# A graph network on one core: inverse root by a power on GpSimd, bias rows added by GpSimd and VectorE

## The chip, the cores and the metric

The kernel runs on one core of a Trainium2 chip. The metric is the device time of one execution in microseconds (us); the kernel before has a median of 6995.06 us over 3 runs (6994.69 to 6996.19). The engines are called TensorE (PE), VectorE (DVE), ScalarE (ACT), GpSimd (POOL) and SyncE (SP).

## The reference

6250 nodes with 256 numbers each, 106250 edges. Four layers, each followed by a residual and a LayerNorm over the 256 numbers:

```python
x = layernorm(x + L0(x))   # h = x @ hamilton(W0); out = segment_sum(edge_weight * h[src], dst)
                           # BatchNorm over the nodes, tanh
x = layernorm(x + L1(x))   # q, k, v = x @ W.T + b; 8 heads, softmax over each node's edges; @ Wo.T + bo
x = layernorm(x + L2(x))   # GAT, 4 heads, + b1; layernorm, relu; GAT, 1 head, + b2
x = layernorm(x + L3(x))   # GCN: segment_sum(dinv[src] * dinv[dst] * (x @ W.T)[src], dst) + b
                           # BatchNorm over the nodes, relu, + x
layernorm = (x - mean) * rsqrt(var + 1e-5)
```

All LayerNorms have the form in the last line (the one inside the GAT also a gain and an offset); the change is about how the `rsqrt` is taken, and about the rows `bq`, `bk`, `bv`, `bo`, `b1`.

## The kernel before

The kernel has a preparation and then five rounds, L = 0 to 4 (the GAT layer takes two rounds). Each round is an **edge pass** and a **node stage**, with a barrier of all five engines between them. In the edge pass GpSimd gathers rows of a table by indirect DMA, 128 edges at a time, TensorE sums them with one-hot matrices, and VectorE adds the sums into `acc`, which keeps the sums of all nodes in SBUF. The change leaves the edge passes alone but for a short preparation of weights at their start.

A node stage walks over the 49 tiles of 128 nodes (`NT`) in steps s; an operation with skew k works on tile n = s - k (`tiles(s, k)`), so each engine's program is a fixed round of operations on different tiles, in the order of its code. No planner is involved. The engines wait for each other by counting semaphores: `rr` (residual added), `var` (mean and variance there), `std` (root taken), `xn` (normalised), `xt` and `xtc` (transposed, copied to SBUF), `pj` (projected), `po` (table row ready), `ps` (stored).

- VectorE: in stages 1 and 2 it divides the sums by the softmax denominators (`pre`, line 1898), then adds the residual or bias (lines 1910, 1914, 1916, 1920), takes statistics (1941, 1936), a reciprocal of ScalarE's root (1933), and normalises (1924; in stages 3 and 4 ScalarE does that at 879, and VectorE makes its offset at 1928).
- ScalarE: `Sqrt` of variance + eps (874), copies of the transposed tile (897) and of the projections out of PSUM (906, 907, 911, 912). In stages 0 and 4 it also applies tanh or Relu to a chunk of four tiles every fourth step (`bend`, 856). Table loads stand in the trace as ACT_TABLE_LOAD.
- TensorE, stage 0: transposes of the layer's result (1185) and of the normalised tile (1208), then the projection onto K and V (1221, 512 columns), a product with `ones_b` and `b3` that adds their bias (1224), the projection onto Q (1227) and its bias (1228). Stage 1: transposes (1191), the product with Wo (1200), the bias row `bo` (1201), transposes (1208), the next layer's projection (1221). A float32 bias is split into three bfloat16 parts by `split_bias` (1386 to 1391), during the edge pass.
- GpSimd, stage 0: rounds the remainder of Q to bfloat16 (725). Stages 1 and 2: zeroes the tile of `acc` (733). Stage 3: adds the row `b2` to the residual tile (721), before VectorE needs it at 1903. Stage 4: nothing.
- SyncE stores the tables and residual tiles, and loads residual tiles in groups of 7.

In stage 0 the remainder of Q goes round three engines: ScalarE's 907 keeps the upper half, VectorE's 1950 subtracts it (semaphore `r0`), GpSimd rounds (725), VectorE's 1945 subtracts again (`qd`), and SyncE stores.

## Time and profile before

| | us |
|---|---|
| median of 3 runs | 6995.06 |
| the profiled execution, its own time | 6978.94 |
| span of that execution | 6977.1 |
| stages 0, 1, 2, 3, 4 (windows read below) | 204, 120, 88, 78, 66 |
| busy over the span: TensorE, VectorE, GpSimd, ScalarE | 4606.5, 4396.6, 4515.6, 2546.8 |

The five node stages together are 556 us, 8% of the span; the busy times over the whole span are those of the edge passes above all. So the rows are read by stage. "Idle before" is the engine's idle time just before the instructions of that group, with what ended it. PEclk is the granted TensorE clock as a share of 2.4 GHz. A row of a window has its stretch, its length, then for each engine the busy us and the count of instructions, then PEclk, the DMA engines' busy share and GB/s. A row of a group has line, engine, operation, output<-input, shapes and count, then busy us and mean ns, then idle before. A timeline row has start, duration, engine, line and operation.

### The profile page before, as it was taken

The numbers are of one execution on the slowest core, as the hardware profiler recorded it, in microseconds if no ns is written. First come the engines' busy times: TensorE is split into PE (matmuls) and PEld (weight loads), VectorE is DVE, ScalarE is ACT, GpSimd is POOL, SyncE is SP. The second block draws the span as 40 slices with busy tenths as digits, with TensorE's granted clock in tenths as the row PEclk, the third lists the DMA queues.
The fourth block names the chain that finished last, engine by engine and source line by source line (L and its number), as shares of the span: only waits on it lengthen the run. The fifth ranks groups of instructions, "written<-read, shape, count | busy, mean of one in ns | idle before, by whom it ended". The sixth has DMA issues, their size and how long they took to land.

```text
span 6977.1 us, 103168 instructions
## 1 busy us (share of the span) xinstructions
PE 4606.5 (66%) x17172; PEld 3026.2 (43%) x17173; DVE 4396.6 (63%) x11645; ACT 2546.8 (37%) x6805; POOL 4515.6 (65%) x4928
## 2 busy tenths in 40 slices
PE   3555555877777777784777777566776735555556
PEld 2444444544444444463444444444444423343333
DVE  5555554558888888874666666655565564444546
ACT  0000000545555655654555555554554540000004
POOL 5777776036666666617777775377777747777770
PEclk8777777988888878896777777777777767777776
DMA  3333335257777777745444444344444543333333
GB/s 86 105 105 105 105 104 102 90 189 221 222 219 222 219 222 223 214 123 149 137 131 132 132 131 92 99 133 135 131 131 136 119 137 105 105 105 105 105 103 89
DMA packets 499186, 962.75 MB, mean 138 GB/s; under 512 B 105403, under 2 KB 296510, under 8 KB 491616
## 3 DMA queue, kind: packets, MB, share of 16 engines
q0 software_dynamic: 240064, 696.46, 36.9%
q1 hardware_dynamic: 258749, 262.93, 11.6%
q14 instruction: 335, 2.74, 0.1%
q8 instruction: 38, 0.62, 0.0%
HBM read 895.74 MB, written 64.63 MB: 138 GB/s over the span
## 4 chain that ended last, share of the span: by engine, by line
PE 36%; POOL 20%; issue 18%; DVE 15%; DVEq 4%; DMA 4%; ACT 3%; ACTq 1%; POOLq 0%; SPq 0%
PE bank L977 21%; POOL ring L707 19%; DVE acc L1439 4%; PE bank L1027 3%; DMA ring<-g_t,stage 2%; PE bank L1221 2%; DVE ring L1651 2%; DVE acc L1436 2%; PE bank L1174 1%; DVE aux L1500 1%; PE bank L1042 1%; DVE ohc L1445 1%; PE bank L1043 1%; PE bank L1044 1%; PE bank L1200 1%
## 5 line engine op out<-in xcount | busy, mean ns | idle before, releaser
L977 PE MATMUL bank<-ring,ohc 128*128 128x256 f32 (+3 forms) x8800 | 3212.4, 517 | 1550.7 <-DMA ring<-xs_t,stage 432.4
L977 PEld LDWEIGHTS bank<-ring,ohc 128*128 128x128 f32 x8800 | 2063.5, 252 | 2500.1 <-issue 1066.7
L1439 DVE TENSOR_TENSOR acc<-acc,bank 128x256 f32 (+2 forms) x3520 | 1485.2, 422 | 1498.3 <-PE bank L977 1368.0
L707 POOL DMA_INDIRECT ring<-g_t,stage x1760 | 1715.7, 975 | 521.7 <-issue 466.2
L707 POOL DMA_INDIRECT ring<-kv_t,stage x880 | 918.2, 1043 | 555.3 <-PE bank L977 325.8
L707 POOL DMA_INDIRECT ring<-in_x,stage x880 | 835.2, 949 | 263.8 <-issue 256.7
L707 POOL DMA_INDIRECT ring<-xs_t,stage x880 | 834.1, 948 | 260.9 <-issue 258.3
L840 ACT ACTIVATE aux<-bank 128x512 f32<-128x512 f32 (+1 forms) x26 | 14.9, 572 | 2225.5 <-PE bank L1163 2225.5
L766 ACT ACTIVATE ohc<-iota,rel_c 128x128 f32<-128x128 f32 x1760 | 557.2, 388 | 67.7 <-PE bank L977 66.6
L812 ACT ACTIVATE cl<-cl 128x1 f32<-128x1 f32 (+3 forms) x111 | 22.5, 203 | 1502.6 <-DVE mx L1644 909.7
L1436 DVE SCALAR_TENSOR_TENSOR acc<-acc,aux,bank 128x264 f32 x880 | 422.9, 481 | 119.9 <-PE bank L977 106.8
L1651 DVE TENSOR_TENSOR ring<-ring 128x1024 f32<-128x1024 f32 (+1 forms) x495 | 487.4, 985 | 14.1 <-issue 5.7
L794 ACT ACTIVATE ring<-ring 128x32 f32<-128x32 f32 x1760 | 378.1, 306 | 0.0
L1445 DVE TENSOR_SCALAR ohc<-iota,rel_c,relx 128x128 f32<-128x128 f32 x883 | 321.0, 364 | 88.3 <-issue 88.3
L827 ACT ACTIVATE ring<-ring 128x256 f32<-128x256 f32 x880 | 353.9, 493 | 2.2
L1448 DVE TENSOR_SCALAR ohc<-iota,rel_c 128x128 f32<-128x128 f32 x883 | 273.9, 310 | 99.4 <-issue 99.4
L769 ACT ACTIVATE ohc<-ohc,onesm 128x512 f32<-128x512 f32 x440 | 317.6, 722 | 32.3
L1042 PE MATMUL bank<-acc,oht 128*128 x880 | 268.2, 305 | 38.7 <-DMA aux<-q_t 30.0
L1500 DVE TENSOR_TENSOR aux<-bank,ring 128x1024 f32<-128x1024 f32 x220 | 267.9, 1218 | 11.6 <-PE bank L1044 10.0
L1491 DVE TENSOR_REDUCE sc<-aux 128x32 f32<-128x1024 f32 x220 | 267.3, 1215 | 2.0
L1043 PE MATMUL bank<-acc,oht 128*128 x880 | 266.7, 303 | 0.0
L1044 PE MATMUL bank<-aux,oht 128*128 128x256 bf16 x880 | 261.0, 297 | 0.0
(299 smaller groups left out, 4954.1 us busy)
## 6 DMA issues: line engine op xcount, KB each, us to landing
aux<-relb_t SPq DMA_DIRECT2D x56, 1024.0 KB
aux<-q_t SPq DMA_DIRECT2D x880, 64.0 KB
relx<-relb_t SPq DMA_DIRECT2D x55, 512.0 KB
ring<-g_t,stage POOLq DMA_INDIRECT x1760, 2.8
x<-ring SPq DMA_DIRECT2D x21, 896.0 KB, 4.2
ring<-x SPq DMA_DIRECT2D x21, 896.0 KB, 9.5
mk<-mk SPq DMA_DIRECT2D x445, 32.1 KB
ring<-in_x,stage POOLq DMA_INDIRECT x880, 2.8
```

The source lines that it names most:

```text
L707: g_.indirect_dma_start(out=rings[L][:, slot, 0:W], out_offset=None, in_=table[L][:, :], in_offset=bass.IndirectOffsetOnAxis(ap=stage[:, s ...
L766: act.activation(ohc[:, at_k + j, :], iota[:, :], ACT.Abs, scale=-1.0, bias=rel_c[:, ds(c * G + 4 * g + j, 1)])
L794: ins = act.activation(part, part, ACT.Copy, scale=rg[:, cset * G + k, po_ + h:po_ + h + 1])
L827: ins = act.activation(row, row, ACT.Copy, scale=rg[:, rset * G + k, 256:257])
L977: return mm(agp[k % AB][:, 0:width], ohc[:, hot, :], rg[:, slot, vo:vo + width], start=True, stop=True)
L1042: mm(to, hot, accb[:, ds(at_ + 2 * AW, D)], start=True, stop=False)
L1043: mm(to, hot, accb[:, ds(at_ + (2 * AW + D), D)], start=False, stop=False)
L1436: v.scalar_tensor_tensor(win, win, same[:, ds(b * G + k, 1)], agp[k % AGP[L]][:, 0:width], ALU.mult, ALU.add).then_inc(p["added"], 1)
L1439: tt(win, win, agp[k % AGP[L]][:, 0:width], ALU.add).then_inc(p["added"], 1)
L1445: ins = v.tensor_scalar(ohc[:, k % 8, :], iota[:, :], rel, ew_c[:, ds(b * G + k, 1)], ALU.is_equal, ALU.mult)
L1500: tt(prod, qe4[r % 2].rearrange("p (t w) -> p t w", t=4), rg[:, rset * G + 4 * r:rset * G + 4 * r + 4, 0:256], ALU.mult).then_inc(p["prod" ...
L1651: return tt(vv, vv, wv, ALU.mult)
```

## The change

- The root moves. GpSimd takes variance + eps (a 128x1 `tensor_scalar`), drains, and raises it to -0.5 (`tensor_tensor` with `half` and `ALU.pow`) in all five stages. ScalarE's `Sqrt` and VectorE's reciprocal go; the steps behind move up by one.
- Stage 0: VectorE adds the bias row of K and V (`kv_b`, 128x512) while it takes the projection out of PSUM; ScalarE's copy (906) and TensorE's product (1224) go. VectorE's last subtraction (1945) moves to GpSimd.
- Stage 1: GpSimd adds `bo` to the residual tile (as stage 3 does with `b2`); TensorE's product (1201) goes. Stage 2: GpSimd adds `b1`, VectorE's 1916 goes, and VectorE's statistics wait for GpSimd.
- `split_bias` is left for the 256 columns of Q alone.

```diff
@@ gpsimd, node stage
-                for n in range(NT):
-                    if L == 3:
+                for s in range(NT + 9):
+                    n = tiles(s, 0)
+                    if n is not None and L == 3:
...
                         g_.tensor_tensor(X49[:, n, :], X49[:, n, :], vrow[:, :], ALU.add).then_inc(q["xb"], 1)
-                    if L == 0:
+                    m = tiles(s, (4, 5, 4, 3, 4)[L])
+                    if m is not None:
+                        pool.wait_ge(q["var"], through("var", L) + m + 1)
+                        pool.nop(nofuse=True)
+                        g_.tensor_scalar(lnst[:, m % 16, 8:9], lnst[:, m % 16, 7:8], EPS, None, ALU.add)
+                        pool.drain()
+                        g_.tensor_tensor(lnst[:, m % 16, 10:11], lnst[:, m % 16, 8:9], half[:, :], ALU.pow)\
+                            .then_inc(q["std"], 1)
+                    m, n = n, tiles(s, 8)
+                    if n is not None and L == 0:
                         pool.wait_ge(q["r0"], n + 1)
                         pool.nop(nofuse=True)
-                        g_.tensor_copy(q_at(n, 1), pr[:, n % 4, :]).then_inc(q["q1"], 1)
+                        g_.tensor_copy(q_at(n, 1), pr[:, n % 4, :])
+                        pool.drain()
+                        if n >= 4:
+                            pool.wait_ge(q[f"ps{n % 4}"], table_stores(L, n - 4))
+                        g_.tensor_tensor(pq[:, n % 4, :], pr[:, n % 4, :], q_at(n, 1), ALU.subtract)\
+                            .then_inc(q["qd"], 1)
...
-                    if L in (1, 2):
+                    n = m
+                    if n is not None and L == 1:
...
+                        g_.tensor_tensor(X[:, n % XS, :], X[:, n % XS, :], vrow[:, :], ALU.add).then_inc(q["xb"], 1)
+                    if n is not None and L in (1, 2):
                         pool.wait_ge(q["pre"], through("pre", L) + n + 1)
                         pool.nop(nofuse=True)
+                        if L == 2:
+                            g_.tensor_tensor(X[:, n % XS, :], X[:, n % XS, :], vrow[:, :], ALU.add)\
+                                .then_inc(q["rr"], 1)
                         g_.memset(acc3[:, n, :], 0.0)
@@ scalar
-                    n = tiles(s, 5 if L == 1 else 3)
-                    if n is not None:
-                        act.wait_ge(q["var"], through("var", L) + n + 1)
-                        act.activation(lnst[:, n % 16, 9:10], lnst[:, n % 16, 7:8], ACT.Sqrt, bias=epsc[:, 0:1])\
-                            .then_inc(q["std"], 1)
...
                         if L == 0:
-                            act.activation(po[:, n % 4, :], ob[:, :], ACT.Copy).then_inc(q["po"], 1)
                             act.activation(q_at(n, 0), banks[6 + n % 2][:, 0:256], ACT.Copy)\
@@ tensor
-                        mm(yb, ones_b[0:96, :], b3[0:96, 0:256], start=False, stop=True).then_inc(q["y"], 1)
...
-                            mm(ob[:, 0:512], ones_b[0:96, :], b3[0:96, 0:512], start=False, stop=True)
@@ vector
-                    n = tiles(s, first + 5)
+                    n = tiles(s, first + 4)
                     if n is not None and L < 3:
+                        dve.wait_ge(q["std"], through("std", L) + n + 1)
                         v.tensor_scalar(slot(n), slot(n), stat(n, 6, 7), stat(n, 10, 11), ALU.subtract, ALU.mult)\
                             .then_inc(q["xn"], 1)
...
-                        v.reciprocal(stat(n, 10, 11), stat(n, 9, 10))
...
+                        if L == 2:
+                            dve.wait_ge(q["rr"], through("rr", L) + n + 1)
                         v.bn_stats(stat(n, 0, 6), slot(n))
-                    n = tiles(s, 11)
+                    n = tiles(s, 8)
                     if n is not None and L == 0:
-                        dve.wait_ge(q["q1"], n + 1)
-                        tt(pq[:, n % 4, :], pr[:, n % 4, :], q_at(n, 1), ALU.subtract)\
-                            .then_inc(q["qd"], 1)
-                    n = tiles(s, 9)
-                    if n is not None and L == 0:
+                        dve.wait_ge(q["pj"], n + 1)
+                        if n >= 4:
+                            dve.wait_ge(q[f"ps{n % 4}"], table_stores(L, n - 4))
+                        tt(po[:, n % 4, :], banks[4 + n % 2][:, :], kv_b, ALU.add).then_inc(q["po"], 1)
                         dve.wait_ge(q["q0"], n + 1)
+                        wait(dve, q["qd"], n - 3)
                         tt(pr[:, n % 4, :], banks[6 + n % 2][:, 0:256], q_at(n, 0), ALU.subtract)\
                             .then_inc(q["r0"], 1)
```

What stands in a row, first on ScalarE in stage 0, before, around one chunk's tanh (856) and the root (874):

```order
L907 ACTIVATE acc<-bank 128x256
L856 ACT_TABLE_LOAD
L856 ACTIVATE acc<-acc,bn 128x512 x2
L874 ACT_TABLE_LOAD
L874 ACTIVATE lnst<-lnst,epsc 128x1
L897 ACTIVATE ring<-bank 128x256
L906 ACTIVATE ring<-bank 128x512
L907 ACTIVATE acc<-bank 128x256
```

And the same place after the change (882 is the tanh, 919 the copy of the transposed tile, 928 that of Q):

```order
L928 ACTIVATE acc<-bank 128x256
L882 ACTIVATE acc<-acc,bn 128x512 x2
L919 ACTIVATE ring<-bank 128x256
L928 ACTIVATE acc<-bank 128x256
L919 ACTIVATE ring<-bank 128x256
L928 ACTIVATE acc<-bank 128x256
```

Both table loads, the root and the 512-column copy are gone from ScalarE's round. VectorE's round in stage 0, before:

```order
L1910 TENSOR_TENSOR ring<-ring,bank 128x256
L1924 TENSOR_SCALAR ring<-ring,lnst 128x256
L1933 RECIPROCAL lnst<-lnst 128x1
L1936 BN_AGGR lnst<-lnst 128x2
L1941 BN_STATS lnst<-ring 128x6
L1945 TENSOR_TENSOR ring<-ring,acc 128x256
L1950 TENSOR_TENSOR ring<-bank,acc 128x256
```

After (1959 is the bias of K and V):

```order
L1924 TENSOR_TENSOR ring<-ring,bank 128x256
L1937 TENSOR_SCALAR ring<-ring,lnst 128x256
L1946 BN_AGGR lnst<-lnst 128x2
L1953 BN_STATS lnst<-ring 128x6
L1959 TENSOR_TENSOR ring<-bank,wmore 128x512
L1962 TENSOR_TENSOR ring<-bank,acc 128x256
```

The reciprocal and the subtraction of 256 columns have left VectorE, the addition of 512 has come. On GpSimd in stage 2 there stood one row before, the memset of 733, 49 times. After the change a round there is:

```order
L728 TENSOR_SCALAR lnst<-lnst 128x1
L730 TENSOR_TENSOR lnst<-lnst,half 128x1
L757 TENSOR_TENSOR ring<-ring,vrow 128x256
L759 MEMSET acc 128x264
L728 TENSOR_SCALAR lnst<-lnst 128x1
L730 TENSOR_TENSOR lnst<-lnst,half 128x1
L757 TENSOR_TENSOR ring<-ring,vrow 128x256
L759 MEMSET acc 128x264
```

The power (730) now stands between VectorE's variance of one tile and its normalisation, and the bias add (757) between VectorE's division and its statistics.

## Rows read from the trace of the kernel before

**Rows 1.** Windows of stages 0-4: busy PE, PEld, DVE, ACT, POOL; PEclk, DMA, GB/s.

```profile
1274.00:1478.00 204.00, 181.21 (x686) 107.26 (x686) 97.81 (x343) 112.90 (x244) 20.96 (x50) 0.92 0.38 127
3028.00:3148.00 120.00, 116.50 (x637) 95.34 (x637) 81.48 (x296) 64.78 (x246) 15.58 (x49) 0.98 0.49 152
4375.00:4463.00 88.00, 68.19 (x294) 48.71 (x294) 76.93 (x296) 65.20 (x245) 15.56 (x49) 0.91 0.22 73
5633.00:5711.00 78.00, 0.00 (x0) 0.00 (x0) 64.11 (x245) 58.50 (x147) 40.26 (x49) 0.50 0.63 211
6905.00:6971.00 66.00, 32.09 (x98) 14.32 (x98) 48.35 (x245) 55.55 (x123) 0.00 (x0) 0.50 0.25 84
```

**Rows 2.** Groups by line, inside stage 0 (1300 to 1460 us).

```profile
L1221 PE MATMUL bank<-wproj,ring 128*128 128x512 f32 x161 | 82.1, 634 | 16.3 <-ACT ring L897 16.3
...
L874 ACT ACT_TABLE_LOAD x9 | 11.5, 1283 | 0.2
```

**Rows 3.** Timeline of stage 0, TensorE: start us, us, engine, line.

```profile
1380.31 0.38 PE L1185 MATMUL bank<-ident,acc 128*128 128x128 f32 x2
...
1382.47 0.38 PE L1224 MATMUL bank<-b,ones_b 96*128 96x512 bf16 x1
...
1382.69 1.03 PE L1227 MATMUL bank<-wproj,ring 128*128 128x256 f32 x4
...
1383.67 0.38 PE L1185 MATMUL bank<-ident,acc 128*128 128x128 f32 x2
```

**Rows 4.** Line 1224: min/median/max ns, first and last start.

```profile
L1224 PE MATMUL bank<-b,ones_b x49: 381/381/634, 1287.8 to 1474.0; 96*128 96x512 bf16 x49
```

**Rows 5.** Timeline of stage 0, VectorE.

```profile
1387.47 0.42 DVE L1910 TENSOR_TENSOR ring<-ring,bank 128x256 f32<-128x256 f32 x1 [0.16 <-issue]
...
1388.60 0.41 DVE L1945 TENSOR_TENSOR ring<-ring,acc 128x256 bf16<-128x256 f32 x1
```

**Rows 6.** Groups by line over the whole run, shapes kept apart.

```profile
L721 POOL TENSOR_TENSOR ring<-ring,vrow 128x256 f32<-128x256 f32 x49 | 40.3, 858 | 59.3 <-DMA ring<-x 59.3
...
L725 POOL CAST acc<-ring 128x256 bf16<-128x256 f32 x49 | 20.6, 420 | 260.4 <-DVE ring L1950 260.4
...
L1854 DVE COPY acc<-bank 128x512 f32<-128x512 f32 x12 | 8.3, 691 | 21.4 <-PE bank L1174 21.4
...
L688 POOL COPY stage<-src_c 128x16 int32<-128x16 int32 x5 | 1.0, 194 | 102.1 <-SPq L389 78.2 <-DVEq L389 23.9
```

**Rows 7.** Timeline of GpSimd at the start; a drain stands before line 642.

```profile
1.72 0.20 POOL L642 MEMSET ident<- 128x128 f32 x1 [0.15 <-issue]
```

**Rows 8.** Timeline of stage 1, TensorE.

```profile
3080.26 0.38 PE L1191 MATMUL bank<-ident,ring 128*128 128x128 f32 x2
...
3082.57 0.38 PE L1191 MATMUL bank<-ident,ring 128*128 128x128 f32 x2
```

**Rows 9.** Timeline of stage 2, VectorE and GpSimd.

```profile
4400.94 0.43 DVE L1898 TENSOR_TENSOR ring<-acc,rden 128x256 f32<-128x256 f32 x1
...
4401.49 0.32 POOL L733 MEMSET acc<- 128x264 f32 x1 [1.30 <-DVE ring L1898]
...
4402.56 0.43 DVE L1898 TENSOR_TENSOR ring<-acc,rden 128x256 f32<-128x256 f32 x1
```

**Rows 10.** Stage 3, VectorE: lines 1903 and 1928; timeline.

```profile
L1903 DVE SCALAR_TENSOR_TENSOR ring<-acc,rden,ring x49: 483/485/1007, 5633.9 to 5699.9; 128x256 f32<-128x256 f32 x49
...
L1928 DVE SCALAR_TENSOR_TENSOR lnst<-lnst x98: 150/152/686, 5640.0 to 6967.9; 128x1 f32<-128x1 f32 x98
...
5672.74 0.68 DVE L1928 SCALAR_TENSOR_TENSOR lnst<-lnst 128x1 f32<-128x1 f32 x1
```

**Rows 11.** Stage 4, VectorE: line 1920; timeline.

```profile
L1920 DVE SCALAR_TENSOR_TENSOR ring<-ring,bank x49: 420/422/423, 6906.3 to 6964.9; 128x256 f32<-128x256 f32 x49
...
6920.57 0.16 DVE L1933 RECIPROCAL lnst<-lnst 128x1 f32<-128x1 f32 x1 [0.60 <-ACT lnst L874]
```

**Rows 12.** Timeline of GpSimd in edge pass 0.

```profile
130.56 0.97 POOL L707 DMA_INDIRECT ring<-in_x,stage  x1 [3.06 <-PE bank L977]
```

More of the change, by code:

```diff
@@ L210, in gnn_kernel @@
         ones_b = sb("ones_b", [96, 128], BF16)
-        epsc = sb("epsc", [128, 1])
+        half = sb("half", [128, 1])
         rows = sb("rows", [1, 7, 144])
@@ L506, in _ @@
                         load(wproj[:, :, 0:256], rowsof(a["L2_gnn_W1"]))
[L507 removed]
+                        load(vrow[:, :], bc(a["L1_gnn_bo"], 256, 128))
                         load(as_b, a["L2_gnn_a1_src"].rearrange("(o h) w -> o (h w)", o=1).to_broadcast([128, 256]))
@@ L667, in _ @@
             g_.memset(ones_b[:, :], 1.0)
-            g_.memset(epsc[:, :], EPS)
+            g_.memset(half[:, :], -0.5)
             by_edge = lambda v: v.rearrange("(o e w) -> o e w", o=1, w=1)
@@ L886, in _ @@
                         act.drain()
-                    n = tiles(s, 8 if L == 1 else 7)
+                    n = tiles(s, 7 if L == 1 else 6)
                     if n is not None and L < 3:
@@ L898, in _ @@
                         ins.then_inc(q["xtc"], 1)
-                    n = tiles(s, 9 if L == 1 else 8)
+                    n = tiles(s, 8 if L == 1 else 7)
                     if n is not None and L < 3:
                         act.wait_ge(q["pj"], through("pj", L) + n + 1)
-                        if n >= 4:
+                        if n >= 4 and L > 0:
                             act.wait_ge(q[f"ps{n % 4}"], table_stores(L, n - 4))
@@ L1199, in _ @@
                         for k in range(2):
-                            mm(yb, preT[:, n % 2, 128 * k:128 * k + 128], wout[:, k, :], start=k == 0, stop=False)
-                        mm(yb, ones_b[0:96, :], b3[0:96, 0:256], start=False, stop=True).then_inc(q["y"], 1)
-                    n = tiles(s, 8 if L == 1 else 7)
+                            ins = mm(yb, preT[:, n % 2, 128 * k:128 * k + 128], wout[:, k, :], start=k == 0,
+                                     stop=k == 1)
+                        ins.then_inc(q["y"], 1)
+                    n = tiles(s, 7 if L == 1 else 6)
                     if n is not None and L < 3:
@@ L1209, in _ @@
                         ins.then_inc(q["xt"], 1)
-                    n = tiles(s, 9 if L == 1 else 8)
+                    n = tiles(s, 8 if L == 1 else 7)
                     if n is not None and L < 3:
@@ L1221, in _ @@
                             ins = mm(ob[:, 0:w1], xv[:, 128 * k:128 * k + 128], wproj[:, k, 0:w1],
-                                     start=k == 0, stop=k == 1 and L > 0)
+                                     start=k == 0, stop=k == 1)
                         if L == 0:
-                            mm(ob[:, 0:512], ones_b[0:96, :], b3[0:96, 0:512], start=False, stop=True)
                             qb = banks[6 + n % 2][:, 0:256]
@@ L1227, in _ @@
                                 mm(qb, xv[:, 128 * k:128 * k + 128], wproj[:, k, 512:768], start=k == 0, stop=False)
-                            ins = mm(qb, ones_b[0:96, :], b3[0:96, 512:768], start=False, stop=True)
+                            ins = mm(qb, ones_b[0:96, :], bq3[0:96, :], start=False, stop=True)
                         ins.then_inc(q["pj"], 1)
@@ L1404, in _ @@
                     dve.wait_ge(q["wc"], 4)
-                    split_bias(768)
-                if L == 1:
-                    dve.wait_ge(q["wl"], loaded(L))
-                    split_bias(256)
-                if L == 2:
+                    tt(bq_t[0:96, :], bq_r[0:96, :], upper(bq_r[0:96, :]), ALU.subtract)
+                    v.memset(bq3[0:96, :], 0.0)
+                    dve.drain()
+                    v.tensor_copy(bq3[0:1, :], upper(bq_r[0:1, :]))
+                    v.tensor_copy(bq3[32:33, :], upper(bq_t[32:33, :]))
+                    tt(bq3[64:65, :], bq_t[64:65, :], upper(bq_t[64:65, :]), ALU.subtract)
+                    dve.drain()
+                    dve.sem_inc(q["w"], 1)
+                if L in (1, 2):
                     dve.wait_ge(q["wl"], loaded(L))
@@ L1927, in _ @@
                     if n is not None and L > 2:
+                        dve.wait_ge(q["std"], through("std", L) + n + 1)
                         v.scalar_tensor_tensor(stat(n, 11, 12), stat(n, 6, 7), -1.0, stat(n, 10, 11), ALU.mult, ALU.mult)\
                             .then_inc(q["nm"], 1)
-                    n = tiles(s, first + 4 if L < 3 else 4)
-                    if n is not None:
-                        dve.wait_ge(q["std"], through("std", L) + n + 1)
-                        v.reciprocal(stat(n, 10, 11), stat(n, 9, 10))
                     n = tiles(s, first + 2 if L != 3 else 2)
```

42 lines of the change are left out of this document (18 added, 24 removed).

## The prediction

> **What bounds the kernel now.** The change touches only the five node stages (stage L follows edge pass L) and two short preparations, so I read the stages one by one. First the busy time by stage [rows 1]: together they are 556 of the 6977.1 us of the span, and what an engine costs there differs from stage to stage. Then, in each stage, the spacing of one instruction from tile to tile, and what it waited for.
>
> Stage 0 is TensorE's, with holes. One undisturbed step, from one pair of transposes to the next, is 1383.67 - 1380.31 = 3.36 us [rows 3]; the stage's mean is (1474.0 - 1287.8) / 48 = 3.88 us [rows 4]. The difference is ScalarE: every fourth step it loads the table for the tanh of the next chunk and then the one for the root, 1.28 us each, 9 of the root's in 160 us and as many of the tanh's, and TensorE's projections stood 16.3 us waiting for ScalarE's copy [rows 2]. The rest is the clock that falls in those holes (0.92 granted in the stage, 0.98 in stage 1 [rows 1]).
>
> Stage 1 is TensorE's without holes: busy 116.5 of 120 us [rows 1], 3082.57 - 3080.26 = 2.31 us for a step [rows 8]. Stage 2 is VectorE's: 76.9 of 88 us [rows 1], 4402.56 - 4400.94 = 1.62 us [rows 9]. Stage 3 has GpSimd and VectorE in each other's way at first and ScalarE at the end: 49 tiles from 5633.9 to 5699.9 [rows 10]. Stage 4 is VectorE's, held up once in four tiles when ScalarE is in its Relu pair and the root comes late (0.60 us [rows 11]); (6964.9 - 6906.3) / 48 = 1.22 us a tile [rows 11].
>
> **The one unknown price: p.** In every stage GpSimd now issues per tile a scalar add on 128x1, a drain, a power on 128x1, and a semaphore wait. Call their time on GpSimd p. No power stands in the trace. A 128x16 copy takes 194 ns [rows 6]; the gap behind a drain is 0.15 us [rows 7]; after a semaphore from VectorE it starts 4401.49 - 4401.37 = 0.12 us later [rows 9]. Low end: two instructions like the copy and the drain, 0.19 + 0.15 + 0.19 = 0.53 us. High end: both as slow as a 128x256 add, 0.86 us [rows 6], so 0.86 + 0.15 + 0.86 + 0.10 = 1.97 us; that is no wall, only the farthest row. I take the add at 0.19 like the copy, since it is as small, and the power at 0.36, nearly double it, for two inputs and a function: 0.19 + 0.15 + 0.36 + 0.10 = 0.80 us. A power costs at least an add, so no gain below 0.53 is in it.
>
> **Stage 0.** The order shows both loads per chunk gone, since no root stands between two tanh any more. TensorE loses the 512-column bias product; its place in the step is 1382.69 - 1382.47 = 0.22 us [rows 3], so the step is 3.36 - 0.22 = 3.14 us. Who could be late next? VectorE: its first four instructions and the reciprocal take 1388.60 - 1387.47 = 1.13 us [rows 5], less 0.08 for the reciprocal; the 512-column add that it takes over from ScalarE is like the 512-column copy from a bank, 0.69 us [rows 6]; the 256-column residual subtraction 0.42; waits about 0.3. That is 2.4 us of 3.14, covered. GpSimd: p + cast 0.42 + drain 0.15 + 128x256 subtraction 0.86 [rows 6] = 2.23 us, covered. ScalarE loses the 512-column copy, and once in four steps still has 1.5 us of tanh, against some 3 us that a turned tile may lie. So 48 x (3.88 - 3.14) = -35.5 us; the ramp ahead of the first projection has one step less and three holes less, -3; the tail -0.5. Together -39 us. If the stage ran with small holes left, -25; more than -42 isn't there.
>
> **Preparation of stage 0's weights.** In edge pass 0 VectorE splits 256 bias columns instead of 768 before it builds its first one-hot tiles, and GpSimd's gathers stood 3.06 us for TensorE right then [rows 12]. Between 0 and -3.06; I take -1.7. In edge pass 1 the split goes entirely, but VectorE then waits for TensorE anyway: 0.
>
> **Stage 1.** TensorE loses a product of 256 columns, half of 0.22: its step is 2.31 - 0.11 = 2.20 us. GpSimd per tile: p + add of the bias row 0.86 [rows 6] + memset 0.32 [rows 9] = 1.98 us, just under. 49 x -0.11 = -5.4; one step and one table load less, -2.3; but the first steps, in which TensorE has half of its work, now go at GpSimd's pace, +3. Sum -5 us. Nothing lies under GpSimd's cover if p is over 2.20 - 1.18 = 1.02.
>
> **Stage 2.** VectorE gives away the bias add (0.42) and the reciprocal and would come down to some 1.2 us. GpSimd, which had a memset of 0.32, now has 0.80 + 0.86 + 0.32 = 1.98 us and sets the pace, because VectorE's statistics wait for GpSimd's add and its normalisation for the power. 45 steps x (1.98 - 1.62) = +16.2; the first steps, in which VectorE has less to do today, go at GpSimd's pace too, +2.5; a step and a table load less, -1.6: +17 us.
>
> **Stage 3.** GpSimd had the add alone, now 0.86 + 0.80 = 1.66 us. 3 x 0.86 + 45 x 1.66 = 77.3 us against 5699.9 - 5633.9 = 66.0: +11.3. ScalarE has lagged behind by the end (the stage went on to 5710), and without its root it no longer does: -5.6. Sum +5.7 us.
>
> **Stage 4.** VectorE's step without the reciprocal is about 1.02 us, and it no longer waits for ScalarE; GpSimd's 0.80 is below. 48 x (1.22 - 1.02) = -9.6, of which I leave 2.6 to a longer chain at the end: -7 us.
>
> **Sum.** -39 - 1.7 - 5 + 17 + 5.7 - 7 = -30 us. The profiled execution had 6978.94 us (span 6977.1); it would have 6949. The median of the runs is 6995.06, 16.1 us above the profiled one, and I carry the same difference: 6965 us. The slope matters more than the point: up to p = 1.02 each 0.1 us costs 9 us (stages 2 and 3), beyond it 18.5 us (stages 1 and 4 join). Break-even is at p = 1.08.
>
> **Contention.** A VectorE instruction with two SBUF inputs, 128x1, has a median of 152 ns, and 0.68 us while GpSimd's adds of stage 3 run [rows 10]. The new kernel puts such adds beside VectorE's 128x256 multiplication in stages 1 and 2. VectorE has room for one such wait (0.5 us) in both, so I price it at 0 there; GpSimd's own add is taken at its contended mean of 0.86. The Trainium skill says the same of two SBUF inputs (GPSIMD Engine Reference, section 8 Key points: GpSimd shares its SBUF interfaces with VectorE, contention with instructions in a 2-port mode or with two SBUF inputs), and by it the normalising tensor_scalar could collide too; with that one as well the sum would be rival 2's.
>
> **Rivals.**
> 1. The power is slow (p of 1.15 to 1.97). Then GpSimd paces stages 1 to 4, and the kernel is slower. At p = 1.4: -30 + 0.22 x 90 + 0.38 x 185 = +60, so 7055 us; it decides from p = 1.08. For it: no row shows a power, and GpSimd's 128x256 add is twice VectorE's. Against: small GpSimd instructions in the trace are all near 0.2 us. Chance 0.27.
> 2. Contention prices both sides: GpSimd's add grows by 0.2 us beside the multiplication and the normalisation, in stages 2 and 3: 45 x 0.2 x 2 = +18 and 6983 us. Chance 0.10.
> 3. Stage 0 doesn't reach TensorE's pace, because the chain bank, add, residual, GpSimd, store goes round late (a step of 3.4): -25 instead of -39, 6979 us. Chance 0.10.
> 4. TensorE's clock. It stood at 0.91 with TensorE busy for 68.2 of 88 us in stage 2, and at 0.50, its lower level of 1.2 GHz, in stage 4 with 32.1 of 66 [rows 1]. At 1.98 us a tile stage 2 leaves TensorE idle more often. Were it all at the lower level, 68.2 / 49 = 1.39 us of busy time a tile would nearly double, up to 0.55 us over GpSimd's pace: 0 to +25, taken at +10, 6975 us. Chance 0.05.
> 5. GpSimd's first power after each pass of gathers pays once, for code that isn't at hand. The first add of stage 3 shows nothing of the kind. Were each of the five first powers late by the longest stop of GpSimd at a pass's start, 3.06 us [rows 12], that is +15, 6980 us. Chance 0.03. The Trainium skill (GPSIMD Engine Reference, section 2.1 Instruction dispatch) states about 6 us for the first call of freshly loaded code, with no instruction in the profile; by its figure the five would be an estimated +30, and the gain gone.
>
> **How the numbers follow.** My forecast (p of 0.53 to 0.98) has 0.45, and 6965 us is its time. A run of this kernel tells 0.2% (14 us) from no change. Faster by that: the forecast, most of 3, half of 2 and 4: 0.57. Within: p from 0.98 to 1.15, the rest of 2 and 3, and 5: 0.15. Slower: rival 1: 0.28. Low end: p = 0.53 gives -30 - 24 = -54, so 6938 us with a little more from stage 0. High end: p = 1.32 gives -10 + 0.30 x 185 = +45, and something of 2 beside it: 7045 us; beyond lies about 0.15.
>
> **What will show it.** Stage 0: spacing of the 512-column projection 3.14 us, no table loads, clock near 1.0. Stage 2: spacing of GpSimd's memset, minus 1.18, is p. Stage 1: spacing 2.20 if p is under 1.02. Stage 3: spacing 0.86 + p. Stage 4: VectorE at 1.02 with no wait for GpSimd. I'm wrong if the power's own row is over some 0.6 us, or if VectorE waits for GpSimd in stage 0.

## The result, and the profile after

The changed kernel takes 6955.86 us (median of 4 runs, 6954.66 to 6957.5), the kernel before 6995.62 us in the same comparison (4 runs, 6994.69 to 6997.11). The ratio is 0.9948, with a 95% interval of 0.9936 to 0.996: faster by some 36 to 40 us. The profiled execution of the changed kernel took 6954.98 us, with a span of 6953.2 us; that is 24 us less than the profiled execution of before, while the medians are 40 us apart. The difference between these two differences is taken up at the end of the experiments.

The totals of the page, for the changed kernel:

```profile
span 6953.2 us, 103674 instructions
...
PE 4547.2 (65%) x17074; PEld 2990.7 (43%) x17075; DVE 4402.0 (63%) x11346; ACT 2448.6 (35%) x6483; POOL 4813.8 (69%) x5565
```

They say little, because the change lies in five stages that make up a twelfth of the span. These are the windows of the five stages, to be set beside [rows 1] (columns as there):

```profile
1275.00:1437.00 162.00, 158.22 (x637) 98.47 (x636) 108.16 (x295) 51.77 (x122) 93.29 (x197) 0.97 0.49 162
2990.00:3105.00 115.00, 110.69 (x585) 92.07 (x584) 89.95 (x244) 54.45 (x195) 89.43 (x196) 0.98 0.50 157
4342.00:4439.00 97.00, 65.41 (x294) 43.35 (x294) 86.70 (x196) 60.98 (x196) 85.34 (x196) 0.94 0.20 66
5612.00:5700.00 88.00, 0.00 (x0) 0.00 (x0) 47.94 (x196) 49.05 (x98) 72.48 (x146) 0.50 0.58 193
6892.00:6950.00 58.00, 31.68 (x98) 13.92 (x96) 44.21 (x196) 45.37 (x73) 38.51 (x98) 0.50 0.33 110
```

The reader sees the exchange at once. In stage 0 TensorE is now busy for 158.22 of 162 us, at a granted clock of 0.97; before it was busy for 181.21 of 204 us at 0.92. In stage 2 GpSimd, which was busy for 15.56 us, is busy for 85.34 of 97, and the stage is longer. VectorE is busy for 86.70 us there although it has 100 instructions fewer than before (196 for 296), so some of its instructions have become longer.

For exact lengths I take a stage from the start of its first instruction (in stage 3, of its first load of residual tiles) to the start of the next edge pass's first load (stage 4: to the end of the span), all in us:

| kernel | stage 0 | 1 | 2 | 3 | 4 | sum |
|---|---|---|---|---|---|---|
| before | 205.9 | 122.8 | 89.4 | 88.5 | 71.6 | 578.2 |
| after | 164.2 | 118.1 | 100.0 | 96.8 | 61.6 | 540.7 |
| difference | -41.7 | -4.7 | +10.6 | +8.3 | -10.0 | -37.5 |

Two stages lose a part of what the other three gain. Now the single steps. In stage 0, TensorE's timeline (start us, us, engine, line):

```profile
1352.02 1.88 PE L1243 MATMUL bank<-wproj,ring 128*128 128x512 f32 x4
1353.74 1.03 PE L1248 MATMUL bank<-wproj,ring 128*128 128x256 f32 x4
...
1355.16 1.02 PE L1243 MATMUL bank<-wproj,ring 128*128 128x512 f32 x2
```

The step is 1355.16 - 1352.02 = 3.14 us, without the product that [rows 3] show between L1221's and L1227's. VectorE waits 0.80 us of each step for TensorE's bank, before its new 512-column add (timeline of VectorE, waits in brackets):

```profile
1351.79 0.69 DVE L1959 TENSOR_TENSOR ring<-bank,wmore 128x512 f32<-128x512 f32 x1 [0.80 <-PE bank L1249]
```

Over the whole stage TensorE's projection waits for nothing (groups of the window 1275 to 1438 us; busy us and mean ns, then the idle time before them):

```profile
L1243 PE MATMUL bank<-wproj,ring 128*128 128x512 f32 x196 | 93.5, 600 | 0.0
```

The 0.0 at the end answers to the 16.3 of [rows 2]. Stage 2, GpSimd and then VectorE, in the same two microseconds:

```profile
4400.48 0.24 POOL L728 TENSOR_SCALAR lnst<-lnst 128x1 f32<-128x1 f32 x1
4400.87 0.57 POOL L730 TENSOR_TENSOR lnst<-lnst,half 128x1 f32<-128x1 f32 x1
4401.40 0.73 POOL L757 TENSOR_TENSOR ring<-ring,vrow 128x256 f32<-128x256 f32 x1
4402.07 0.32 POOL L759 MEMSET acc<- 128x264 f32 x1
4402.36 0.25 POOL L728 TENSOR_SCALAR lnst<-lnst 128x1 f32<-128x1 f32 x1
...
4401.12 0.43 DVE L1912 TENSOR_TENSOR ring<-acc,rden 128x256 f32<-128x256 f32 x1
4401.47 1.06 DVE L1937 TENSOR_SCALAR ring<-ring,lnst 128x256 f32<-128x256 f32 x1
4402.46 0.16 DVE L1946 BATCH_NORM_AGGREGATE lnst<-lnst 128x2 f32<-128x6 f32 x1
```

GpSimd has no gap: its step is 4402.36 - 4400.48 = 1.88 us, in four pieces from start to start: 0.39 (scalar add and drain), 0.53 (power), 0.67 (row add), 0.29 (memset). So p, the price that the prediction hung on, is 0.39 + 0.53 = 0.92 us. VectorE has no gap either, because its normalisation L1937 lasts 1.06 us. Its length has a pattern: it ends 0.40 us after GpSimd's add (4402.53 against 4402.13), and so it does, within 0.01 us, in 44 of the stage's 49 tiles. So VectorE seems to begin the work only when GpSimd's add is done. Which of the two engines sets the pace is a question for the experiments. In stage 3 it can be read at once, since VectorE waits there for GpSimd's row in 46 of the 49 steps:

```profile
5650.99 0.48 DVE L1917 SCALAR_TENSOR_TENSOR ring<-acc,rden,ring 128x256 f32<-128x256 f32 x1 [0.68 <-POOL ring L723]
```

### The profile page after: what moved, and what is told of

The parts are those of the page before. It is cut to its first block, busy times and chain, and to the rows that moved or that the text cites. A ratio compares the mean times of both kernels' runs of the same rounds, so it can differ in the third digit from the quotient of the medians.

```text
span 6953.2 us, 103674 instructions
## 1 busy us (share of the span) xinstructions
PE 4547.2 (65%) x17074; PEld 2990.7 (43%) x17075; DVE 4402.0 (63%) x11346; ACT 2448.6 (35%) x6483; POOL 4813.8 (69%) x5565
## 4 chain that ended last, share of the span: by engine, by line
PE 36%; POOL 20%; issue 18%; DVE 14%; DVEq 4%; DMA 4%; POOLq 2%; ACT 1%; SPq 0%; ACTq 0%
PE bank L998 21%; POOL ring L708 18%; DVE acc L1453 4%; PE bank L1048 3%; DMA ring<-g_t,stage 2%; PE bank L1243 2%; DVE ring L1665 2%; DVE acc L1450 2%; DVE ohc L1459 1%; POOLq L729 1%; DVE aux L1514 1%; PE bank L1195 1%; PE bank L1063 1%; PE bank L1064 1%; PE bank L1065 1%
```

## The experiments

The theory from the profile, **theory 1**: in stages 2 and 3 GpSimd's own time per tile sets the pace. **Theory 2**, its rival: VectorE sets it, since its instructions are blocked while GpSimd adds. (Each expectation numbers its own theories anew.) For stage 0 the question is how the gain divides between the root, with its table loads, and the bias product, with ScalarE's 512-column copy and VectorE's last subtraction that went with it. Times and ratios are against the kernel before, measured beside each run; stage lengths are given for stages 0 to 4.

### Only the root goes back

ScalarE takes the square root and VectorE the reciprocal again, in all five stages; the steps behind move back by one. The rest is the changed kernel's.

```diff
+ROOT_ACT = (0, 1, 2, 3, 4)
...
-                    if m is not None:
+                    if m is not None and L not in ROOT_ACT:
...
+                        act.activation(lnst[:, n % 16, 9:10], lnst[:, n % 16, 7:8], ACT.Sqrt, bias=epsc[:, 0:1])\
+                            .then_inc(q["std"], 1)
...
+                        v.reciprocal(stat(n, 10, 11), stat(n, 9, 10))
```

> The changed kernel with the root back on ScalarE (and the reciprocal on VectorE) in all stages; the bias adds stay where the change put them. Stage lengths run from a stage's first instruction to the next pass's first load; before and after they were 205.9 and 164.2, 122.8 and 118.1, 89.4 and 100.0, 88.5 and 96.8, 71.6 and 61.6 us. Theory 1 (GpSimd's own time paces stages 2 and 3 of the changed kernel, 0.92 us of it the root): stage 0 gets its table loads back, about 195 (only the 0.22 us a tile of the bias product stay won); stage 1 about 119; stage 2 at about 1.35 us a tile, some 80; stages 3 and 4 as before, 88 and 72. Sum about -24 against before. Theory 2 (VectorE is blocked while GpSimd adds 128x256, and that paces stage 2): stage 2 stays at 1.85 to 1.9 us a tile, about 100, sum -4.

Measured: 6954.83 us, ratio 0.9944 (0.9927 to 0.9961). Stages: 183.5, 118.9, 75.1, 88.4, 71.6, sum 537.5 us. Stage 2, VectorE and then GpSimd:

```profile
4400.29 0.43 DVE L1922 TENSOR_TENSOR ring<-acc,rden 128x256 f32<-128x256 f32 x1
4400.63 0.41 DVE L1948 TENSOR_SCALAR ring<-ring,lnst 128x256 f32<-128x256 f32 x1
...
4401.11 0.39 DVE L1969 BATCH_NORM_STATS2 lnst<-ring 128x6 f32<-128x256 f32 x1
4401.58 0.42 DVE L1922 TENSOR_TENSOR ring<-acc,rden 128x256 f32<-128x256 f32 x1
...
4400.86 0.76 POOL L761 TENSOR_TENSOR ring<-ring,vrow 128x256 f32<-128x256 f32 x1 [0.27 <-DVE ring L1922]
4401.57 0.31 POOL L763 MEMSET acc<- 128x264 f32 x1
```

The same add on GpSimd stands in the stage, and the step is 4401.58 - 4400.29 = 1.29 us. GpSimd waits for VectorE (0.27), and the normalisation takes 0.41 us although the two overlap: here it begins before the add (4400.63 against 4400.86). Theory 2 in its plain form falls: an add on GpSimd doesn't set VectorE's pace where GpSimd has room. The run doesn't say what a blocked instruction would cost, since none is blocked in this step. With the add alone on GpSimd stage 2 would have **gained** 14.3 us over before (89.4 to 75.1); the root on top of it cost 24.9.

Over the whole kernel this gives what the change gives: a ratio of 0.9944 against 0.9948, and 537.5 us of stages against 540.7. Moving the root wins in stages 0 and 4 (19.3 and 10.0 us) what it loses in stages 2 and 3 (24.9 and 8.4). The expected sum of -24 us came out at -40.7.

Stage 0 came out at 183.5 where 195 was expected. ScalarE's timeline shows why it is not shorter, the two table loads:

```profile
1355.45 1.28 ACT L886 ACT_TABLE_LOAD   x1
...
1358.29 1.28 ACT L904 ACT_TABLE_LOAD   x1
```

In the groups of the whole stage, the last number is the idle time of TensorE before the projection:

```profile
L1253 PE MATMUL bank<-wproj,ring 128*128 128x512 f32 x196 | 94.9, 607 | 13.9 <-ACT ring L929 13.9
```

TensorE still stood 13.9 us for ScalarE here, in the whole stage.

### Only the root is moved

The kernel before, with only the root on GpSimd; both bias products, the row additions and the copies stay.

```diff
+                        g_.tensor_scalar(lnst[:, m % 16, 8:9], lnst[:, m % 16, 7:8], EPS, None, ALU.add)
+                        pool.drain()
+                        g_.tensor_tensor(lnst[:, m % 16, 10:11], lnst[:, m % 16, 8:9], half[:, :], ALU.pow)\
+                            .then_inc(q["std"], 1)
...
-                        act.activation(lnst[:, n % 16, 9:10], lnst[:, n % 16, 7:8], ACT.Sqrt, bias=epsc[:, 0:1])\
...
-                        v.reciprocal(stat(n, 10, 11), stat(n, 9, 10))
```

> The kernel before with only the root moved to GpSimd; all bias rows and the last subtraction of stage 0 stay where they were. Both theories: stage 0 without holes at 3.36 us a tile, about 176 (before 205.9); stage 1 about 121, stage 4 62. Theory 1: stage 2 at VectorE's 1.54 us a tile, since GpSimd needs 0.92 + 0.29 = 1.21, about 86; stage 3 at GpSimd's 1.64, about 97. Theory 2 says the same of stage 2, as no add of GpSimd runs there. Sum about -35 against before: of the change's gain nearly all is this one part.

Measured: 6971.34 us, ratio 0.9968 (0.9955 to 0.998). Stages: 176.7, 123.6, 92.2, 97.6, 61.1, sum 551.2 us. Stages 0, 3 and 4 are as expected; stage 1 was expected at 121, stage 2 at 86 and the sum at -35 us, where -27.0 was measured, so this part is far from the whole gain. In stage 0 the root gives 29.2 us of the 41.7 and the moves around the bias product the other 12.5. With TensorE's extra product in place its step is 3.35 us (timeline of stage 0):

```profile
1352.27 1.88 PE L1228 MATMUL bank<-wproj,ring 128*128 128x512 f32 x4
1353.99 0.38 PE L1231 MATMUL bank<-b,ones_b 96*128 96x512 bf16 x1
...
1355.62 1.45 PE L1228 MATMUL bank<-wproj,ring 128*128 128x512 f32 x3
```

The other order, bias first (the run above), gave 22.4 and then 19.3 us. The two parts add up to 51.6 if each is done alone, to 41.7 together. A reason that fits, argued and not tried by itself: moving the bias also takes the 512-column copy of 0.60 us a tile from ScalarE, so the holes that the loads tear are smaller there, and the root has less to close.

Stage 1 shows that its gain of 4.7 us is the bias product alone: with the root only, it is 123.6 us. Stage 4's 10 us are the root alone (61.1).

### The row of stage 2 goes back to VectorE, then that of stage 3 too

This is the edit for stage 2. The second run has it too, and in stage 3 VectorE adds `vrow` in place of GpSimd, with the steps behind one later.

```diff
-                        if L == 2:
-                            g_.tensor_tensor(X[:, n % XS, :], X[:, n % XS, :], vrow[:, :], ALU.add)\
-                                .then_inc(q["rr"], 1)
...
+                        if L == 2:
+                            tt(slot(n), slot(n), vrow[:, :], ALU.add).then_inc(q["rr"], 1)
```

> The changed kernel with the add of b1 in stage 2 back on VectorE. Stage 2 at VectorE's 1.54 us a tile, about 86 instead of 100; the rest as in the changed kernel. Against the changed kernel -14 us. If stage 2 were paced by something else (TensorE's clock, ScalarE's two activations), it stays over 95.

Measured: 6952.71 us, ratio 0.994 (0.9924 to 0.9957). Stage 2 is 92.2 us, where 86 was expected. VectorE and then GpSimd there:

```profile
4401.49 0.42 DVE L1909 TENSOR_TENSOR ring<-acc,rden 128x256 f32<-128x256 f32 x1
4401.83 0.42 DVE L1927 TENSOR_TENSOR ring<-ring,vrow 128x256 f32<-128x256 f32 x1
4402.16 0.58 DVE L1936 TENSOR_SCALAR ring<-ring,lnst 128x256 f32<-128x256 f32 x1
...
4403.22 0.42 DVE L1909 TENSOR_TENSOR ring<-acc,rden 128x256 f32<-128x256 f32 x1
...
4401.26 0.22 POOL L728 TENSOR_SCALAR lnst<-lnst 128x1 f32<-128x1 f32 x1 [0.39 <-DVE lnst L1945]
4401.63 0.71 POOL L730 TENSOR_TENSOR lnst<-lnst,half 128x1 f32<-128x1 f32 x1
```

Here GpSimd has room (it waits 0.39 us for VectorE) and the step is VectorE's, 4403.22 - 4401.49 = 1.73 us. The miss is contention in both directions: the power lasts 0.71 instead of 0.57 us beside VectorE's multiplication and addition, and the normalisation lasts 0.58 instead of 0.41. It ends 0.40 us after the power (4402.74 against 4402.34), and 43 of the 49 tiles show the same within 0.01 us, as behind the add. Without this stretch VectorE's step would be 1.56, and 49 x 0.17 = 8.3 us is more than the 6.2 missing. So VectorE's blocked instruction does cost time in this arrangement, in which GpSimd isn't the bound. Before the change, with a memset alone on GpSimd, the same VectorE work and a reciprocal took 1.62 us [rows 9]. Against the changed kernel the stages give 7 us, where 14 were expected, and in time the two can't be told apart: the intervals overlap.

The Trainium skill has the rule behind it (GPSIMD Engine Reference, section 8 Key points): GpSimd shares its SBUF interfaces with VectorE. The rows agree, and add the size: here a power on 128x1 costs the VectorE instruction beside it 0.17 us.

> The same, and the add of b2 in stage 3 also on VectorE. Stage 3: VectorE 1.03 + 0.35 = 1.38 us a tile, GpSimd 0.92, ScalarE 1.08; about 84 instead of 96.8 if GpSimd's time paced it. Against the changed kernel -26 us together. If the stores of 12.8 MB pace stage 3 (211 GB/s before), it stays near 88.

Measured: 6942.93 us, ratio 0.9927 (0.9911 to 0.9944). Stage 3 is 85.8 us (about 84 expected), 11.0 less than in the changed kernel and 2.7 less than before; VectorE's step is 1.38 us and GpSimd waits for it. Against the changed kernel the stages give 18 us, where 26 were expected; what is missing is stage 2's part. VectorE and then GpSimd in stage 3:

```profile
5650.74 0.48 DVE L1908 SCALAR_TENSOR_TENSOR ring<-acc,rden,ring 128x256 f32<-128x256 f32 x1
5651.14 0.42 DVE L1913 TENSOR_TENSOR ring<-ring,vrow 128x256 f32<-128x256 f32 x1
...
5652.12 0.48 DVE L1908 SCALAR_TENSOR_TENSOR ring<-acc,rden,ring 128x256 f32<-128x256 f32 x1
...
5650.87 0.78 POOL L724 TENSOR_TENSOR lnst<-lnst,half 128x1 f32<-128x1 f32 x1
5651.88 0.22 POOL L722 TENSOR_SCALAR lnst<-lnst 128x1 f32<-128x1 f32 x1 [0.23 <-DVE lnst L1941]
```

### The power as a multiplication

```diff
-                        g_.tensor_tensor(lnst[:, m % 16, 10:11], lnst[:, m % 16, 8:9], half[:, :], ALU.pow)\
+                        g_.tensor_tensor(lnst[:, m % 16, 10:11], lnst[:, m % 16, 8:9], half[:, :], ALU.mult)\
```

> The changed kernel with GpSimd's power replaced by a multiplication of the same two 128x1 operands, which leaves the inverse root out, so that the values are no longer the reference's. If it is the power as an operation that makes GpSimd's part of a tile 0.92 to 0.95 us long (theory 1), a multiplication takes some 0.15 to 0.2 us instead of 0.57, the step of stage 2 falls by about 0.37 us from 1.88 to 1.5 (stage 2 from 100 to about 82 us) and that of stage 3 from 1.64 to about 1.3 (97 to about 81, or to VectorE's 86). If it is the call with its drain and wait (theory 2), a multiplication takes as long as the power and both stages stay within 3 us. Stages 0, 1 and 4 stay within 2 us by both, since GpSimd waits there for the others.

In this run and the next three the whole kernel was slower: TensorE's mean granted clock was 0.70 in place of 0.77, and the kernel before took 8492.02 us beside this run; so the times can't stand beside the others. The node stages can: before measured 206.1, 123.6, 89.2, 88.3 and 71.6 us there, within 0.8 us of its first profile. Measured for the multiplication: ratio 0.9894 (0.9868 to 0.992), stages 164.2, 119.0, 80.4, 78.9, 61.3. The line of the multiplication (min/median/max ns):

```profile
L730 POOL TENSOR_TENSOR lnst<-lnst,half x245: 189/190/378, 1504.7 to 8362.1; 128x1 f32<-128x1 f32 x123
```

One step of stage 2, GpSimd and then VectorE, timeline:

```profile
5096.82 0.19 POOL L730 TENSOR_TENSOR lnst<-lnst,half 128x1 f32<-128x1 f32 x1
5096.97 0.72 POOL L757 TENSOR_TENSOR ring<-ring,vrow 128x256 f32<-128x256 f32 x1
5097.63 0.31 POOL L759 MEMSET acc<- 128x264 f32 x1
5097.92 0.20 POOL L728 TENSOR_SCALAR lnst<-lnst 128x1 f32<-128x1 f32 x1
5098.27 0.19 POOL L730 TENSOR_TENSOR lnst<-lnst,half 128x1 f32<-128x1 f32 x1
...
5097.32 0.65 DVE L1912 TENSOR_TENSOR ring<-acc,rden 128x256 f32<-128x256 f32 x1
...
5097.89 0.40 DVE L1937 TENSOR_SCALAR ring<-ring,lnst 128x256 f32<-128x256 f32 x1
```

0.19 us against 0.57: the power as an operation is what is long. The step is 5098.27 - 5096.82 = 1.45 us instead of 1.88, and stage 2 is 100.0 - 80.4 = 19.6 us shorter, stage 3 17.9. Shortening one GpSimd instruction by 0.38 us shortens the stage by about as much a tile. For stage 2 this alone is no proof of theory 1, because VectorE's stretch shrank as well: its normalisation is back at 0.40 us, and what meets the add is now its multiplication (0.65 instead of 0.43). What speaks for theory 1 there is that in the changed kernel GpSimd's own four pieces fill the 1.88 us without a wait, at the lengths that they have elsewhere (the add 0.73 us, against 0.76 where VectorE set the pace), while VectorE's row without its stretch of 0.65 is 1.23 us: its stretch lies inside the time that GpSimd needs in any case. Stages 0, 1 and 4 stay within 1 us, as expected: GpSimd is not their bound. The scalar add with its drain, and a short instruction in the power's place, still cost 0.35 + 0.15 = 0.50 us a tile.

> The kernel of e5_multiply once more, the inverse root left out. The power as an operation is what is long (theory 1): stage 2 about 82 us and stage 3 about 81 to 86. The call with its drain and wait (theory 2): both within 3 us of 100 and 97.

Measured, at a granted clock of 0.705: one time of 8285.45 us; stages 164.4, 119.4, 80.6, 79.1, 61.3. The same.

### A mixture of the two kernels

Stage 2: the root on ScalarE, the row on GpSimd. Stage 3: the root on GpSimd, the row on VectorE. The rest is the changed kernel's.

```diff
+ROOT_ACT = (2,)
...
-                        g_.tensor_tensor(X49[:, n, :], X49[:, n, :], vrow[:, :], ALU.add).then_inc(q["xb"], 1)
...
+                        if L == 3:
+                            tt(slot(n), slot(n), vrow[:, :], ALU.add)
```

> The changed kernel with two stages set otherwise: in stage 2 ScalarE takes the square root and VectorE the reciprocal, as before the change, and GpSimd only adds its row; in stage 3 GpSimd takes the root and VectorE adds the row. Stages 0, 1 and 4 are the changed kernel's. If the stages are independent of one another (theory 1), each keeps the length that it had where it was last seen so: 164, 118, 75, 86 and 62 us, 505 in all, 36 less than in the changed kernel, so the time is about 6920 us. If a stage's gain is given back in the edge pass behind it, or by a table load of ScalarE at the stage's two ends (rival), the stages are the same and the passes longer, and the time is 6935 to 6950.

Measured at the granted clock of 0.70: 8409.46 us against 8492.02, ratio 0.9905 (0.9883 to 0.9926); stages 164.5, 118.0, 76.3, 85.1, 61.8, sum 505.7 us. The stages are as expected; the time had to be measured again without the slower passes.

> The kernel of e7_mixed once more, since TensorE's granted clock was 0.70 over the whole of that run where it was 0.93 or more in the runs before. If the stages are independent (theory 1): 164, 118, 75, 86 and 62 us, 505 in all, and about 6920 us; if the edge passes give it back (rival), 6935 to 6950.

The granted clock was 0.70 again: 8296.4 us against 8371.16, ratio 0.9913 (0.989 to 0.9936); stages 164.2, 118.5, 76.0, 85.2, 61.8.

> The kernel of e7_mixed again, whose node stages took 505.7 us with a granted clock of 0.70 over the edge passes (before: 578.8). At the clock of the first runs (0.93) the stages should be the same, 505 us, and the time about 6920 us, 0.990 of the kernel before (theory 1); if the passes give the gain back (rival), 6935 to 6950.

(The 0.93 in this text and in the one before is wrong: the mean granted clock of the first runs was 0.77, and 0.766 was granted here.) Measured: 6934.05 us (4 runs, 6932.19 to 6935.4) against 7002.3, ratio 0.9903 (0.9886 to 0.9919); stages 164.1, 118.2, 76.0, 85.9, 61.8, sum 506.0 us. The interval lies wholly below that of the changed kernel (0.9936 to 0.996): this version is faster than both. The ratio is the 0.990 that was expected; the 6920 us were not reached, because the kernel before takes 7 us more here, and because the gain is 68 us in time where the stages give 72 to 76. So the edge passes give at most a few back (they sum to 6427.8 us here, 6423.3 in the kernel before on the same chip). The stages are independent of one another: each keeps, within 1 us, the length that it had where it was last set so.

### Why the profiled executions are only 24 us apart

The edge pass behind stage 1 took 1223.9 us in the first profile of before and 1234.8 in that of after. Either the change lengthens it, or the first profile was short there by chance.

> The kernel before, unchanged, profiled once more. In its first profile the edge pass 2 took 1223.9 us, in every kernel profiled since between 1234.0 and 1242.3, and the node stages 578.2 us. If that pass was short by chance in that one execution (theory 1), it comes out at 1234 to 1242 us here, the node stages at 577 to 580 and the span at 6985 to 6997. If something in the change lengthens the pass by 11 us (theory 2), it is 1224 again and the span 6977.

> The kernel before once more. If edge pass 2 was short by chance in the first profile (theory 1): pass 2 1234 to 1242 us, the node stages 577 to 580, the span 6985 to 6997. If the change lengthens the pass (theory 2): 1224 and 6977.

Both fell among the slower executions (8515.22 and 8341.32 us) and say nothing on the pass, which took 1562.9 and 1509.2 us; the node stages summed to 578.8 and 579.7 us, so they repeat.

> The kernel before once more, at the clock of the first runs if it is granted. If edge pass 2 was short by chance in the first profile (theory 1): pass 2 1234 to 1242 us, the node stages 577 to 580, the span 6985 to 6997. If the change lengthens the pass (theory 2): 1224 and 6977.

Measured: 7006.93 us, span 7005.1, at a granted clock of 0.768. The pass took 1239.0 us, as theory 1 has it. The node stages took 581.8 us, 209.0 of them stage 0 (before 205.9), and the other passes are some 9 us longer together than in the first profile; so the span is 8 us over the expected range. The windows over the pass, of before in its first profile, of after, and of before in this one:

```profile
3152.00:4374.00 1222.00, 829.68 (x3132) 560.72 (x3132) 776.06 (x1731) 673.12 (x1354) 902.09 (x934) 0.74 0.47 127
```

```profile
3106.00:4340.00 1234.00, 822.53 (x3132) 558.44 (x3132) 774.64 (x1731) 670.34 (x1352) 912.30 (x936) 0.74 0.46 126
```

```profile
3162.00:4400.00 1238.00, 823.00 (x3132) 555.12 (x3132) 776.29 (x1731) 673.14 (x1354) 917.70 (x935) 0.74 0.47 126
```

With unchanged code the pass is long (and 1241.3 us in the mixture on the same chip), so the change isn't what lengthens it. The fifth number, GpSimd's busy time with its gathers, goes with the length: 902 us for the short pass, 912 and 918 for the long ones, for nearly the same number of instructions. Why the gathers took 1% less in that one execution is open.

The slower executions differ in the passes too. The same pass in the first of them:

```profile
3612.00:5174.00 1562.00, 877.77 (x3132) 585.04 (x3132) 773.74 (x1731) 673.82 (x1354) 917.25 (x936) 0.68 0.37 100
```

The pass is 339 us longer than in the first profile, but TensorE's busy time in it grew by 48 us only, and the DMA engines moved 100 GB/s in place of 127. So the lower clock alone doesn't make these executions slow; what does is open.

## Why the prediction was right

The forecast was 6965 us, the result 6955.86, and it lies in the range of 6938 to 7045. The sign came out in all five stages, and the engine that was to set the pace in each. The sizes are off by 0.3 to 6.4 us, and a part of the closeness is luck, since two prices on GpSimd were wrong in opposite directions. Step by step:

- **p.** Forecast 0.80 us, measured 0.92. The power was taken at 0.36 us because it is "nearly double" a small copy; it lasts 0.57 and holds the engine 0.53. The scalar add with its drain was 0.39, against 0.19 + 0.15. The wait priced at 0.10 costs nothing where GpSimd is the bound, since the signal is there before.
- **The row add and the memset.** These were priced too high, at 0.86 and 0.32 us; from start to start they are 0.67 and 0.29. The 0.86 was the mean of the adds in the stage 3 of before. So the step of stage 2, forecast at 1.98, is 1.88 us, and the step of stage 3, forecast at 1.66, is 1.64: two errors, in p and in the add, that cancel, which was luck. Stage 2, forecast at +17, measured +10.6. Stage 3, forecast at +5.7, measured +8.3: the step is as forecast, so the 5.6 us taken off for ScalarE at the end were for the most part not there. With the add at 0.67 the break-even lies higher than the 1.08 given, at a p of about 1.2 us (an estimate from these rows).
- **Stage 0.** Forecast 3.14 us a step and -39 us; measured 3.14 and -41.7. The mechanism holds in all its parts: no table load in the steps, the projection waits for nothing, the clock at 0.97, and VectorE waits for TensorE's bank and not for GpSimd. GpSimd's work there, forecast at 2.23 us, is about 0.92 + 0.40 + 0.15 + 0.76 = 2.23 us.
- **Preparation.** Forecast -1.7 us, measured +0.3: edge pass 0 took 1274.4 and then 1274.7 us. This step failed. The 3.06 us of [rows 12] was one gather's wait, and nothing showed that VectorE's split was what it waited for.
- **Stage 1.** Forecast -5, measured -4.7, with the step of 2.20 us. The run with only the root moved shows that nothing of it comes from the root alone.
- **Stage 4.** Forecast -7, measured -10.0. VectorE's tile is (6941.8 - 6892.4) / 48 = 1.03 us, as forecast; the 2.6 us kept back for a longer chain at the end are not there. The row below shows the first and last start of its 49 operations.

```profile
L1932 DVE SCALAR_TENSOR_TENSOR ring<-ring,bank x49: 420/421/422, 6892.4 to 6941.8; 128x256 f32<-128x256 f32 x49
```

- **From profile to median.** The forecast is in effect the median of before less 30 us. The steps above come to -37.5 + 0.3 = -37.2 us, so 7.2 of the 9.1 us between forecast and result are theirs; the medians fell by 2.6 us more than that, which no stage shows. The 16.1 us carried had no cause named: 11 to 15 us of it is the short edge pass of one profile, and the changed kernel's profiled execution and its median differ by 0.9 us. The gap did no harm because it only led back to the median of before; as a forecast of the profiled execution, 6949 us was 6 us too low.
- **Contention.** It was priced at 0 in stages 1 and 2 because VectorE had room. The place was right and the size was not: not one wait of 0.5 us, but 0.65 us on the normalisation (0.41 to 1.06) in nearly every tile of stage 2. By the Trainium skill's rule (GPSIMD Engine Reference, section 8 Key points) the prediction allowed that the tensor_scalar collides, and L1937 does. It costs nothing only because GpSimd's 1.88 us are longer than VectorE's need; rival 2's 18 us didn't come, for GpSimd's add was not lengthened (0.73 us). Where VectorE set the pace, such a collision did cost time (stage 2 at 92.2 us instead of 86).
- **Rivals.** 1 (a slow power) was half true: the power's own row of 0.57 us is just below the 0.6 given as the sign of being wrong, in stage 3 it is 0.61, and p did not reach 1.08. 3 didn't come. 4: the granted clock in stage 2 was 0.94 in the window (0.91 before), it didn't fall. 5: in each of the five stages the first power starts 0.38 to 0.40 us after its scalar add, against 0.36 to 0.40 later on, and lasts no longer than 0.76 us, the line's maximum; so nothing is paid once there:

```profile
L730 POOL TENSOR_TENSOR lnst<-lnst,half x245: 557/568/756, 1278.1 to 6944.7; 128x1 f32<-128x1 f32 x123
```

What the prediction did not see: in stage 2 the two moves are not of one kind. The row add alone on GpSimd is worth -14 us, and the root alone costs +3; together they cost 11. Both fit GpSimd one at a time and not together. It priced the bundle and not its parts, and so missed the mixture, whose ratio is 0.9903 against 0.9948. Nor did it see that, once the rows are moved, moving the root in all five stages gives nothing over the whole (0.9944 without it, 0.9948 with it).

## What to carry to other kernels

When a bundle of moves goes to one engine, price each move in each stage, with the pace of the engine that receives it. A move is free as long as the receiver waits, and costs its full length from there on; here the same power was worth -29 us in stage 0, where it removes table loads, and +25 in stage 2, where it came on top of an add.

A stretched instruction looks harmful and may cost nothing. While GpSimd paced stage 2, with no wait and at its usual lengths, VectorE's normalisation of 1.06 us was hidden; when VectorE paced it, a stretch of 0.17 us a tile cost the stage some 6 us. So ask first which engine has no wait at its own unstretched lengths.

Forecast a difference, and take it off the median of the kernel before. Its profiled execution can be short by chance; here it was 11 to 15 us short in a pass that the change doesn't touch. The lengths of such parts show whether a profile is a typical one.

## What the runs showed of the hardware

- A power on 128x1 on GpSimd lasts 0.57 us, a multiplication of the same operands 0.19 us, a scalar add 0.22 us; from the scalar add's start over a drain to the next start it is 0.35 to 0.39 us.
- VectorE's normalisation (tensor_scalar, 128x256) lasts 0.41 us alone, 0.58 when it begins during GpSimd's power, and 1.06 when it begins beside GpSimd's 128x256 add. In both cases it ends 0.40 to 0.41 us after GpSimd's instruction, one whole length of its own, so it looks blocked until then and not slowed. Its batch statistics, with one input, stay at 0.39 us beside the same add.
- The multiplication of two SBUF inputs on VectorE (128x256) lasts 0.65 instead of 0.43 us when it begins during that add.
- The reverse also shows: the power lasts 0.71 us beside VectorE's 128x256 instructions with two SBUF inputs in stage 2, and 0.78 in stage 3.
- Some executions were a fifth slower, with a mean granted clock of 0.70 in place of 0.77: the kernel before then took 8341 to 8515 us, and the edge pass behind stage 1 took 1509 to 1563 us instead of 1224 to 1239, at 100 GB/s instead of 127 in the one looked at. The node stages, with 0.92 granted in stage 0 of the kernel before in both cases and 0.97 in that of the kernels with both moves, kept their lengths within 2 us.
